# Four attention layers unrolled into a pipeline of 16 items that shares its slots with code-book look-ups

## What is computed

```python
# x: (1, 2048, 512)
x = layernorm(x + attn(x))
x = layernorm(x + ffn(x))

def attn(x):                       # DIM 64, 4 layers, DFF 256
    h = x @ Win.T + bin
    for each layer:
        y = silu(layernorm(h) * ln1_w + ln1_b)
        y = real part of the convolution over time of y with p**t, plus last_conv * p**(t+1)
        h = h + y * sc_lin
        y = silu((layernorm(h) * ln2_w + ln2_b) @ W1.T + b1) @ W2.T + b2
        h = h + y
    return (layernorm(h) * lnl_w + lnl_b) @ Wout.T + bout

def ffn(x):                        # inner size 1376; codebook: 8192 rows of 8 numbers
    Wg, Wu, Wd = (codebook[idx].reshape(rows, -1) for idx in (idx_gate, idx_up, idx_down))
    return (silu(x @ Wg.T) * (x @ Wu.T)) @ Wd.T
```

## Time and profile before

| | us |
|---|---|
| median of 3 runs | 1604.21 |
| lowest, highest | 1602.64, 1605.93 |
| time of the profiled execution | 1605.78 |
| its span, first to last instruction | 1604.0 |

### The profile page before, as it was taken

One profiled execution on the slowest core, in us unless ns is written; L12 is line 12 of the kernel. 1 busy time (PEld: TensorE's weight loads), 2 busy tenths in 40 slices (PEclk: granted clock), 3 DMA queues, 4 the chain that ended last, 5 costly groups with the idle time before them and its releaser, 6 DMA issues.

```text
span 1604.0 us, 18430 instructions
## 1 busy us (share of the span) xinstructions
PE 1514.5 (94%) x6437; PEld 1119.0 (70%) x6437; DVE 1305.2 (81%) x2417; ACT 260.6 (16%) x448; POOL 768.2 (48%) x706
## 2 busy tenths in 40 slices
PE   4798898989999999999999999999999999999996
PEld 3332332357778888788888788887888887888874
DVE  3925325389999988999988999879999889998866
ACT  2533434350000010000000000100000000010004
POOL 4666556565655555445554456455454545520000
PEclk8857757659999999999999999999999999999998
DMA  7100000104544433454433555423454345444212
GB/s 160 21 3 3 2 3 3 29 3 86 97 90 90 86 77 59 79 89 88 83 65 66 86 90 87 76 62 77 89 88 82 66 65 87 90 86 74 57 34 105
DMA packets 138892, 107.52 MB, mean 67 GB/s; under 512 B 43757, under 2 KB 134645, under 8 KB 138806
## 3 DMA queue, kind: packets, MB, share of 16 engines
q1 hardware_dynamic: 112756, 98.56, 30.0%
q0 software_dynamic: 22016, 2.86, 5.1%
q10 hardware_dynamic: 4034, 4.98, 1.0%
HBM read 101.42 MB, written 4.92 MB: 66 GB/s over the span
## 4 chain that ended last, share of the span: by engine, by line
PE 82%; DVE 11%; issue 4%; ACT 2%; SPq 1%; DMA 0%; ACTq 0%; DVEq 0%
PE bank L453 40%; PE cand L453 40%; DVE one_hot L888 4%; DVE xn L698 2%; DVE g L830 1%; DVE chosen L909 1%; PE cand L570 1%; DVE small L698 0%; DVE x L698 0%; ACT x L381 0%; SPq L207 0%; DVE stats L865 0%; ACT rs L332 0%; SPq L217 0%; ACT L332 0%
## 5 line engine op out<-in xcount | busy, mean ns | idle before, releaser
L275 POOL DMA_INDIRECT stage_down<-in_L_ffn_codebook,idx_down x688 | 765.5, 1113 | 649.8 <-DMA stage_down<-in_L_ffn_codebook,idx_down 464.4
L453 PE MATMUL cand<-one_hot,book 128*128 128x512 f32 x2816 | 720.3, 398 | 10.2 <-DVE one_hot L888 9.9
L453 PEld LDWEIGHTS cand<-one_hot,book 128*128 128x128 f32 x2816 | 522.6, 188 | 145.3 <-DVE one_hot L888 21.0
L888 DVE TENSOR_SCALAR one_hot<-bc,low_of 128x512 fp32r<-128x512 uint16 x1408 | 591.2, 482 | 1.1 <-DMA bc<-index_parts 1.1
L909 DVE SCALAR_TENSOR_TENSOR chosen<-bc,high_of,cand 128x1024 fp32r<-128x1024 uint16 x352 | 449.4, 1277 | 83.6 <-PE cand L453 82.5
L453 PEld LDWEIGHTS bank<-chosen,adder 128*128 128x128 f32 x1408 | 214.6, 188 | 40.2 <-DVE chosen L909 9.0
L453 PE MATMUL bank<-chosen,adder 128*128 128x256 f32 x1408 | 223.4, 280 | 7.8 <-DVE chosen L909 7.8
L453 PE MATMUL bank<-x1t_hi,wg 128*128 128x512 f32 (+1 forms) x352 | 130.3, 394 | 0.5 <-ACT wg L396 0.5
L453 PE MATMUL bank<-x1t_hi,wu 128*128 128x512 f32 (+1 forms) x352 | 126.1, 394 | 0.0
L453 PE MATMUL bank<-wd,act_hi 128*128 128x512 f32 (+1 forms) x328 | 103.6, 397 | 0.3
L396 ACT ACTIVATE wg<-bank 128x256 fp32r<-128x256 f32 x44 | 16.9, 385 | 430.2 <-PE bank L453 430.2
(11 more groups left out here) (181 smaller groups left out, 1005.3 us busy)
## 6 DMA issues: line engine op xcount, KB each, us to landing
bc<-index_parts SPq DMA_DIRECT2D x352, 256.0 KB, 4.6
stage_down<-in_L_ffn_codebook,idx_down POOLq DMA_INDIRECT x688
x<-in_L_attn_x ACTq DMA_DIRECT2D x4, 1024.0 KB, 9.1
out_x<-x SPq DMA_DIRECT2D x16, 256.0 KB, 2.0
index_parts<-parts_t SPq DMA_DIRECT2D x11, 64.0 KB
w_in<-in_L_attn_W ACTq DMA_DIRECT2D x2, 256.0 KB, 8.0
idx_down<-in_L_ffn_idx_down SPq DMA_DIRECT2D x1, 344.0 KB, 6.1
sq<-in_L_ffn_idx_up SPq DMA_DIRECT2D x1, 320.0 KB, 10.7
```

What stands on the lines that cost most here:

```text
L275: pool.indirect_dma_start(stage_down[k % RING][:, q, j * CS:(j + 1) * CS], None, a["L0_ffn_codebook"], bass.IndirectOffsetOnAxis(ap=idx_do ...
L453: return pe.matmul(dst, lhs, rhs, start=start, stop=stop)
L888: last = v.tensor_scalar(one_hot[quad % 2][:, q, :], bc[quad % 4][:, 0, :], low_of[:, q:q + 1], None, ALU.is_equal)
```

## The change

- **Layers.** The 4 layers by 4 chunks are 16 items, and the hardware loop is gone: 22 slots are written out. Slot t holds the first norm, silu and scan of item t, the matmul back and h's addition of item t - 1, the second norm and W1 of item t - 2, and W2 of item t - 3. Slots 16 to 19 hold the last norm of one chunk each, slots 17 to 20 output matmul, addition and normalisation of four tiles, slots 18 to 21 transposes and x1t_hi, x1t_lo of four tiles, all through PSUM bank 2 (four banks took turns before).
- **h** has 128 rows, with the mean already taken off: the centring is folded into the weights (`wint`, `w2t`, `mix`, by the matrix `centre`) once, so that the layers have no centring matmul, and ACT squares h in SBUF.
- **Look-ups.** Eight quads are begun in the set-up and two more in each slot, 52 ahead of the feed-forward tiles, whose 300 left quads are shared out by `quads_of`: 28, 31, 31, then 30 each. The last tile's 32 quads are 96 wide instead of 128. The weights live in a ring of 20 groups. `add_up` of a quad comes behind the candidates of the next in every place, over the border of tiles too. The phase with look-ups of tile 0 alone is gone.
- **Buffers.** `bc` has three buffers instead of four (`BCS`), the stage of the down weights three instead of four (`RING`).
- **Set-up.** The first tile's indices are loaded and split first, the code book is split before the layers, weight copies went from DVE to ACT, and `mix` and `turn` are made for all four layers at once.

```diff
-    SHARES = (8, 5)
-    TURN_DOWN = (4, 3)
-    FIRST_DOWN = 13
-    RING = 4
-    BURST = 4
+    WRING = 20
+    BCS = 3
+    RING = 3
+    BURST = 4
+    EARLY = 8
+    PER_SLOT = 2
+    SLOTS = ITEMS + 6
+    AHEAD_QUADS = EARLY + PER_SLOT * SLOTS
+    SHARES = (7, 5)
+    TURN_DOWN = (4, 3)
+    FIRST_DOWN = 13
+
+    def quads_of(k):
+
+        first = AHEAD_QUADS
+        for n in range(k + 1):
+            most = min(ALL_QUADS, 4 * WRING + QUADS * n)
+            left = FULL - n
+            count = min(most - first, -(-(ALL_QUADS - first) // left))
+            if n == k:
+                return range(first, first + count)
+            first += count
...
@@ SP
-                if quad >= 4:
-                    sp.wait_ge(s["chosen_made"], quad - 3)
+                if quad >= BCS:
+                    sp.wait_ge(s["chosen_made"], quad - BCS + 1)
...
@@ ACT, layers
+            for t in range(SLOTS):
+                i1, i2 = t, t - 2
+                if 0 <= t - 1 < ITEMS:
...
+                    act.wait_ge(s["h_mid"], t)
...
+                    act.activation(sq2[(t - 1) % 2], h[:, c * C:(c + 1) * C], ACT.Square).then_inc(s["sq2_made"], 1)
+                if i1 < ITEMS + NC:
+                    act.wait_ge(s["var1"], i1 + 1)
...
+                    root(rs1, bank[1][:, :]).then_inc(s["rs1_made"], 1)
...
@@ PE, layers
+            for t in range(SLOTS):
+                quad = EARLY + PER_SLOT * t
+                if t < ITEMS and t % NC:
...
+                    mm(bank[2][:, 0:1], turn[:, t // NC, :], g[:, C - 1:C]).then_inc(s["rotated"], 1)
+                if 0 <= t - 1 < ITEMS:
...
+                    mm(bank[0][:, :], mix[:, (t - 1) // NC, :], d).then_inc(s["mixed"], 1)
+                if t < ITEMS + NC:
...
+                    mm(bank[1][:, :], mean_p[:, :], sq1).then_inc(s["var1"], 1)
+                if 0 <= t - 2 < ITEMS:
...
+                    mm(bank[2][:, :], mean_p[:, :], sq2[t % 2]).then_inc(s["var2"], 1)
...
+                candidates(quad)
+                add_up(quad - 1)
+                if 0 <= t - 3 < ITEMS:
...
+                    for k in range(FK):
+                        done = mm(bank[0][:, :], w2t[:, (t - 3) // NC, k, :], ff[:, k, :], k == 0, k == FK - 1)
+                    done.then_inc(s["ff_back"], 1)
+                if 0 <= t - 2 < ITEMS:
...
+                    for k in range(FK):
+                        done = mm(bank[1 + k][:, :], w1t[:, (t - 2) // NC, k * P:(k + 1) * P], g2)
+                    done.then_inc(s["spread"], 1)
...
+                add_up(quad)
+                if 0 <= t - ITEMS - 1 < NC:
+                    for n in range(TPC):
+                        project((t - ITEMS - 1) * TPC + n)
+                candidates(quad + 1)
...
@@ feed-forward slots, PE
-                    if slot < QUADS:
-                        candidates(k + 1, slot)
-                    if 0 < slot < QUADS:
-                        add_up(k + 1, slot - 1)
...
+                    if slot < len(quads):
+                        candidates(quads[slot])
+                        add_up(quads[slot] - 1)
```

More of the change, by code:

```diff
@@ new lines, in build @@
+            iota_low = st("iota_low", [P, LT], I32)
+            iota_m = st("iota_m", [P, 1], I32)
+            parts_t = [st(f"parts_t{b}", [JP, 2, P], U16) for b in range(3)]
+            rows = st("rows", [ROWS, P])
+            cosp = st("cosp", [P, L, 10])
+            sinp = st("sinp", [P, L, 10])
+            small = st("small", [P, 12, L])
+            sgn = st("sgn", [P, 1])
+            perm = st("perm", [P, P])
+            turn_a = st("turn_a", [P, L, P])
+            w1_in = st("w1_in", [P, L * FK, D])
@@ new lines, in build @@
+            state = at("state", [P, 1])
+            woutt = at("woutt", [D + 1, V])
+            cols = at("cols", [P, L, LAYER_COLS])
+            last_cols = at("last_cols", [P, 4])
+            mean_p = at("mean_p", [P, P])
+            centre = at("centre", [P, P])
+        sq1, rs1, xn, y, u, g, d = (work[:, n, :] for n in range(7))
+        sq2 = [work[:, 7 + b, :] for b in range(2)]
+        rs2, g2 = work[:, 9, :], work[0:D, 10, :]
+        ff = work[:, 11:13, :]
+        hn = [work[0:D + 1, 3 + b, :] for b in range(2)]
@@ L588, in candidates @@
-            def candidates(n, slot):
-                quad = n * QUADS + slot
+                    done = mm(dst[:, :], wint[:, k, :], xt[c % 2][:, k, :], k == 0, k == KT - 1)
+                done.then_inc(s["h_sum"], 1)
+            def candidates(quad):
+                nw = 4 * width(quad)
                 pe.wait_ge(s["one_hot_made"], quad + 1)
@@ L595, in candidates, with add_up @@
                     for q in range(LT):
-                        last = mm(cand[quad % 2][:, m, :], book[m][:, q, :], one_hot[quad % 2][:, q, :], q == 0, q == LT - 1)
-                last.then_inc(s["candidates"], 1)
-            def add_up(n, slot):
-                quad = n * QUADS + slot
+                        done = mm(cand[quad % 2][:, m, 0:nw], book[m][:, q, :], one_hot[quad % 2][:, q, 0:nw], q == 0, q == LT - 1)
+                done.then_inc(s["candidates"], 1)
+            def add_up(quad):
+                nw = width(quad)
@@ L602, in add_up @@
                 pe.wait_ge(s["chosen_made"], quad + 1)
[L603 removed]
+                if quad % 4 == 0 and quad:
                     pe.wait_ge(s["picked_kept"], quad // 4)
                 for jj in range(4):
[L606 to L608 removed]
@@ new lines, in _ @@
+            turn_x(1, bank[2])
+            pe.wait_ge(s["parts_kept"], 1)
+            turn_x(2, bank[0])
+            pe.wait_ge(s["x_kept"], 1)
+            turn_x(3, bank[1])
+            pe.wait_ge(s["w_in"], 64)
+            for half, (dst, free) in enumerate(((bank[2], 2), (bank[0], 3))):
+                pe.wait_ge(s["x_kept"], free)
+                for n in range(4):
+                    done = pe.transpose(dst[0:D, n * P:(n + 1) * P], w1_in[:, half * 4 + n, :], ident[:, :])
+                done.then_inc(s["turned_w"], 1)
```

1016 lines of the change are left out of this document (561 added, 455 removed).

## The result

| | us |
|---|---|
| before, median | 1604.41 (1602.64 to 1605.93) |
| after, median | 1632.70 (1630.18 to 1634.93) |
| ratio | 1.0176, 95% interval 1.0158 to 1.0194 |
| profiled execution of after, and its span | 1634.93, 1633.1 |

Slower by 1.8%, inside the range and 11 us under the forecast of 1644: of the 40 us more that were forecast 28 came. A ratio can differ from the quotient of the medians by 0.2%, and it leaves out executions over 1.5% above a kernel's quickest, which there are in one experiment, the fourth stage buffer beside the fourth bc buffer. The page of after: busy time of the engines, the granted clock in 40 slices, the chain that ended last by engine and by line, and the landing of the broadcasts.

The account below looks back on a forecast made before the run. Three broadcast buffers were taken to bound the feed-forward tiles at 3.78 us a quad; 100 + 204 + 110 + 1177 + 52.7 = 1643.7, as a median about 1644 us, 2.5% slower, range 1595 to 1700.

Parts of the forecast that it names:

- set-up: Up to the last choose before the layer slots: bound by DVE, 100 us after added look-ups, book, tables and index split.
- slots 17 to 21: Output stage x1, four tiles per slot through PSUM bank 2, clock between half and full: 110 us, bounds 101 and 119.
- feed-forward tiles: 300 quads with three broadcast buffers: 1177 us against 1101.3 before, 76 longer though 20 quads fewer.
- The ring law: Feed-forward tiles: with three buffers two quads share landing, one-hots and choose, 2P = 4.70 + 2.86 = 7.56, P = 3.78 us.
- The last tile: Tile 9, narrow: landing of 192 KB taken as 4.4 us between 3.1 and 4.65, P = 3.35, 111 us for the tile.
- Layer slots: Steady slots 3 to 15: DVE 10.96 us plus a 1.3 us wait for rs1, 12.3 us each; PE fits with 10.9.
- The clock: PE in the layer slots: 2.4 GHz, since mix, means and look-ups now have 128 rows.
- rival 2: Half clock in the layer slots: PE's 10.9 become 21.5, a slot 22.5, total 1787 us; chance 0.05.
- rival 3: Overlap doesn't hold: hand-overs among four engines make a layer slot 15 us instead of 12.3, total 1682; chance 0.09.
- rival 4: Set-up, tail and landing (4.3 instead of 4.65) all at their low ends: 1595 to 1607 us; chance 0.06.
- Rival 1: Broadcast landing hidden, deciding at 3.2 us: PE sets the feed-forward tiles, 1035 us, total 1502; chance 0.11.
- The gathers: POOL's three-deep stage ring for down weights: tile 3's wait costs gathers 40 us, yet they stay ahead of need.

## Why the prediction was right

| term | forecast | measured |
|---|---|---|
| set-up | 100 | 93.7 |
| slots 0 to 16 | 204 | 198.4 |
| slots 17 to 21 | 110 | 100.4 |
| feed-forward tiles | 1177 | 1188 |
| end | 52.7 | 52.6 |
| sum | 1643.7 | 1633.1 |

The mechanism came as forecast, and the sum is closer than its terms: everything ahead of the tiles was 21.5 us too high (they start at 392.6, not near 414), the tiles 11 too low, and half of the error cancels. That is luck.

- **The ring law** carried the verdict, and three runs show it: 7.56 forecast and 7.55 to 7.62 measured with two buffers, 3.78 and 3.81 to 3.86 with three (tiles 4, 6 and 8), hidden with four. The even tiles were 2% dearer than their term, 573 us against 564, which is most of the 11. Odd tiles 3 and 7 came at 125.1 and 126.1 against 124.6, tile 1 at 126.9 against 128.4. Tile 5 took 122.0, since its quads 208 to 223 landed quickly; that wasn't foreseen.
- **The last tile** was mis-sized most of the single tiles: 111 against 115.05. The landing of 192 KB was taken as 4.4, and it is 4.7, as long as that of 256 KB. The upper bound was the right value: less width gave nothing. With 4.7 the same sum makes 114.
- **Set-up** was 6.3 too high. DVE is busy for 48.21 of its last 50.70 us, so it does bind; no run tells which of the added items was overpriced.
- **Layer slots** were 12.0 against 12.3, the wait for rs1 1.11 against 1.3. The run that puts the root first shows that it lies on the path. PE's work was mis-sized, 10.9 against 11.5, which cost nothing here and set the bound in that run. Leaving out the drain behind a table load was right: with it a slot was to be 13.7, and the root starts 0.01 us after its load here (223.63 against 222.34 + 1.28).
- **Slots 17 to 21** were 10 too high: slot 17 took 17.2 against 18, slots 18 to 20 24.8, 22.1 and 22.8 against 25 each, slot 21 13.6 against 17. The clock was between its two levels, 0.80, as taken, so the rest of the error is overlap: transposes and hi and lo parts hide more behind the adds than the sum allowed. That is an argument, not a run.
- **The clock** in the layer slots was 0.99; rival 2 (half clock) is out. The slots of 12.0 put rival 3 (15 us) out. Of rival 4's low ends the set-up came in (93.7), the landing and the end did not. With three buffers or four a steady layer slot is 12.0, so the landing does have cover there, as taken.
- **Rival 1** (landing hidden, 1502) was out at a landing of 4.6. As a price it was good: its tiles of 1035 are those of the run with four buffers and bursts of eight; that run's 1490 against 1502 is a set-up 6 us dearer and slots 16 us cheaper than summed. The Trainium skill's rule of double-buffering, on which it leaned (Trainium Kernel Development and Optimization, Best Practices), holds for three buffers with the one landing and not with the other. The estimate of 2.6 us from DMA: Bandwidth & Descriptors (the Trainium skill), Anatomy of one DMA, isn't reached even by the quick landings of 3.2; that section's fit is for transfers that GpSimd issues, and these are SyncE's.
- **DVE's wait** was to be 200 us or more: 208.6. PE's idle time in even tiles was to be 15 to 20% and is 13% in tile 4. DVE's share in the tiles of before was read as 92 to 96%; in tile 1 it is 88%, and nothing hangs on it.
- **The gathers** "still ahead": true at this pace (the run with four stage buffers), and only at this pace. With four bc buffers they are the next bound: the tiles take 62 us less with bursts of eight (1097 to 1035), of which 44 are left after the dearer set-up.

The two halves of the change can now be told apart. Everything but the three bc buffers is worth 70 us (1604 to 1534), and 114 if the gathers are let keep up (1490). The missing buffer costs 99 us, and 143 against the run with bursts of eight; the second number is for two edits, since three buffers with bursts of eight weren't run.

## What to carry to other kernels

A buffer taken away from a ring is judged by a ring law: (landing + time from first use to release) / (buffers - 1 when use and release are one item apart), against the pace of the engine that binds; an idle wait of 1 us in the old trace says nothing about the margin. After each bound that is lifted, look at the next queue, here the gathers, which cost 44 us of the expected gain: it was not only outrun but slowed. And look at landings one by one and not at the median alone: the odd 16 led to a layout in DRAM worth as much as the buffer (1494 against 1490), though the two together gave no more.

## What the runs showed of the hardware

- A broadcast of 256 KB lands in 4.6 us when its source is two stretches of 1 KB 32 KB apart, in 3.2 when they lie together; 192 KB with stretches 24 KB apart in 4.7, together in 3.2. Between these, neither the bytes nor the number of packets set it: 192 KB in 256 packets did both.
- 16 quads at one place in DRAM landed in 3.2 in the old layout as well, and which quads these are changed with a shift of the tensor by 64 KB (208 to 223, then 176 to 191).
- Gathers in bursts of eight lengthened the set-up from 94.1 to 106.1 us; begun with the 192nd they left it as it was.
- With two, three or four buffers a broadcast lands in the same 4.6 us, with one or two of them under way, while the means over the span go from 37 to 72 GB/s. The gathers beside them aren't so steady: a burst of four was waited for 2.70 us with three buffers, 2.99 with four, and 2.20 with three and the layout in one stretch.
- A table load of 1.28 us is followed by its root after 0.01 us.
